# Cross-attention and MXFP8 FFN on one core: constants first, 8 warming matmuls, ScalarE's row statistics in halves, a later wait in the last down product, new orders

## The chip, the cores and the metric

One core of a Trainium2 chip runs the whole program. TensorE does the matmuls and reads instructions from its own queue, as do VectorE (DVE), ScalarE (ACT), GpSimd (POOL) and SyncE (SP), which issues most of the DMAs. The metric is the time of one execution on the device, in microseconds (us). The kernel before took 611.59 us (median of 3 runs, 611.04 to 611.65).

## The reference, cut to what matters

The input `x` is 4 x 512 x 512, the context 4 x 512 x 256, everything float32. A cross-attention without learned values is added to `x`, then a gated feed-forward network in which every matrix and every activation is rounded to float8 in blocks of 32 (quantised and dequantised):

```python
query = einsum('bnc,dc->bnd', ctx, Wq) + bq          # d = 128
key   = einsum('bnc,dc->bnd', ctx, Wk) + bk
attention = softmax(einsum('bnd,bmd->bnm', query, key), axis=-1)
x = x + einsum('bln,bmn->blm', layernorm(x), attention)

def mx_dequant(t):                                   # blocks of 32 along the last dimension
    scales = maximum(max_abs(blocks) / 448, 1e-30)
    return (blocks / scales).astype(float8_e4m3fn).astype(float32) * scales
def mx_linear(x2d, w): return mx_dequant(x2d) @ mx_dequant(w).T

gate, up = mx_linear(layernorm(x), gate_w), mx_linear(layernorm(x), up_w)   # 512 -> 2048
out = x + mx_linear(silu(gate) * up, down_w)                                # 2048 -> 512
```

## The kernel before, in words

**Stages.** The attention runs per batch entry b = 0..3 in 128-row tiles. `project(b, i)` makes queries (i = 0) or keys (i = 1) with 2 float32 matmuls; a float32 matmul stands in the profile as 2 records. `energies(b, nt)` makes one 128x512 tile of scores with 1 matmul. DVE's `row_max` and ACT's `exponential` turn it into unnormalised probabilities; `row_sum(b)` inverts the four sums; ACT's `weigh(b, nt)` scales an identity matrix by them. `turn_probs(b, nt)` multiplies the probabilities by that diagonal, which transposes and normalises them (4 matmuls, 128 columns each); `take_probs` copies the result to SBUF. `attend(b, lt)` multiplies by the rows of `x` (4 matmuls, 512 columns), and DVE's `add_attended` adds it to `x`, using the layernorm statistics that ACT makes in `row_means(b)` and `row_variances(b)`. The second layernorm is `attended_means` (DVE), `attended_variances` (ACT), a centring by DVE (`center`) or ACT (`center_by_scalar`), and `rows_scale`, `rows_round`, `rows_dequant` (DVE).

The weights come as 12 units of 1 MB: units 0 to 7 are gate and up for 4 column groups c, units 8 to 11 are the down matrix. Each is rounded by DVE (`unit_reduce`, `unit_scale`, `unit_round`, `unit_dequant`) with help of ACT (`unit_magnitude`, `unit_rescale`), and split into a high and a low float16 part: ACT writes the high part (`unit_hi`), GpSimd's accumulating DMA (`unit_rest`) forms the remainder, ACT writes the low part (`unit_lo`), and SP's transposing DMAs (`turn_unit_hi`, `turn_unit_lo`) put both in place. The normalised rows go the same way (`rows_hi`, `rows_rest`, `rows_lo`, `turn_rows_hi`, `turn_rows_lo`), and so do the hidden rows.

`product(r, c)` makes gate and up of row tile r (0..15) and column group c, in three float16 passes each (high x high, high x low, low x high): 24 matmuls. ACT's `silu_of` and DVE's `hidden_of` combine them. `down(r)` makes an output tile with 48 matmuls. `down_last()` makes tile 15 in two halves of 256 columns, so that the first half can be added and stored while the second is computed.

**What sets the order.** No planner runs with the kernel: each engine's instructions stand in an order written out by hand in the source, and an engine runs them strictly in this order. Semaphores hold an instruction back until its inputs are there; whatever stands behind it on that engine waits as well. The 8 PSUM banks are shared by a written list, `bank_uses`: a bank's next user waits until its last user has been read (`take_bank`, `bank_left`).

**Start.** DVE writes a block of zeros. TensorE runs `keep_zeros(18)` (L758): 18 float16 matmuls of those zeros into a spare bank. It then waits for both constant DMAs (L331 weights and biases, L332 identity) and for the context. SP issues in this order: the two halves of unit 0 (L325, L328), context 0 (L335), the two constant DMAs, context 1, unit 1, rows 0, context 2, unit 2, context 3, columns 0 and so on.

**End.** `down_last()` waits for both the high part (`hT_in[0]`) and the low part (`hT_in[1]`) of row 15 before its first matmul, then computes all of half 0 and all of half 1. DVE's `add_last` (L1612) and `store_last` (L364) follow each half.

Of the kernel before, what the change touches and what calls it, by code (L numbers as in the profile page):

```python
# [9 lines left out]
ALU = mybir.AluOpType  # L10
# [3 lines left out]
P = 128  # L14
# [18 lines left out]
def xattn_ffn(nc, xrows, xcols, ctxT, consts, units, out):  # L33
# [35 lines left out]
        ("p0.0 p2.0 t0.0 e2.1 a1.3 t3.3 a3.2 u3.1 g4.1 u6.2 u0.1 g1.1 g4.2 u7.1 d1 u13.0 g13.3 g8.3 g10.3 u15.0"  # L69
         " u15.3").split(),  # L70
        ("p0.1 e1.0 t0.2 e2.2 t2.0 e3.2 t3.1 g0.0 g2.1 u4.0 g3.2 g0.2 u0.3 u3.3 g7.2 g8.0 g9.1 u9.3 d3 u10.3 g15.1"
         " d10 d13").split(),
        ("p1.0 e1.1 a0.0 a0.2 t1.1 t1.3 a1.2 a2.2 u1.0 g6.0 u4.1 u3.2 g5.3 u1.1 g4.3 u7.2 g8.1 g9.2 u11.0 g12.0"
         " g14.0 g14.2 g12.2 u13.1 g12.3 g10.1 g11.3 d8 d11").split(),
        ("e0.0 e1.2 a0.1 a0.3 e3.1 t3.0 g1.0 a3.3 u2.1 g5.0 g5.1 u0.2 g1.2 u4.2 g7.3 u8.0 u9.1 g11.0 g11.2 g12.1"
         " u14.0 g14.3 g13.0 u13.2 u8.2 u10.2 d6 d9 d12").split(),
        ("e0.1 p2.1 t0.1 t0.3 e2.3 t2.1 e3.3 t3.2 a3.0 g2.0 g6.1 g2.2 u5.1 u5.3 u1.2 g7.0 g2.3 g9.0 g9.3 g11.1 d4"
         " u15.1 d14").split(),
        ("e0.2 e1.3 t1.0 t1.2 a1.1 t2.3 a2.1 u3.0 g3.1 u6.1 g6.2 g0.1 u6.3 g3.3 g7.1 u2.3 u9.0 g10.0 u11.1 u12.0"
         " g14.1 u14.2 u12.2 g13.2 u12.3 u10.1 u11.3 g15.2 d15").split(),  # L80
        ("e0.3 p3.0 e3.0 a2.3 a3.1 u2.0 g4.0 u2.2 u5.2 g0.3 u1.3 u7.0 d0 u10.0 u11.2 u12.1 u14.1 u14.3 g13.1 u13.3"
         " u8.3 d5 d7 g15.3").split(),
        ("p1.1 e2.0 p3.1 a1.0 t2.2 a2.0 g3.0 u0.0 u6.0 u5.0 g5.2 g6.3 g1.3 u4.3 u7.3 u8.1 u9.2 d2 g8.2 g10.2 g15.0"
         " u15.2").split(),
# [4 lines left out]
    logged = (0,)  # L89
    hidden_by_vector = (7, 8, 9, 10, 11, 12, 13, 14, 15)  # L90

    with ExitStack() as stack:
# [55 lines left out]
        idf = late[:, 1540:1540 + P]  # L148
        xsum, xnmean, xssq, xlog, xrstd, nmax, esum, rsum = [late[:, 1680 + RT * n:1680 + RT * (n + 1)] for n in range(8)]
        xTf = [h[:, 0:LT, 1536:2048], h[:, 0:LT, 1024:1536]]  # L150
# [22 lines left out]
        def hrow(r):  # L173
            return h[:, r % SLOTS, :]

# [34 lines left out]
        xmean_ready = sem("xmean_ready")  # L210
        ymean_ready = sem("ymean_ready")
# [106 lines left out]
        def _(sp):  # L318
# [121 lines left out]
            load_ctx(3)  # L440
            load_columns(0)
            load_rows(1)
            load_rows(2)
            load_columns(1)
# [3 lines left out]
            load_rows(3)  # L448
            load_unit(3)
            store_rows(0)  # L450
            load_columns(2)
# [20 lines left out]
            turn_rows_lo(1)  # L472
            turn_unit_hi(4)
            turn_unit_lo(4)
# [21 lines left out]
            turn_unit_hi(10)  # L496
            reload_rows(2)
            turn_unit_lo(10)
            turn_unit_hi(11)
            sp.wait_ge(*hidden_rest_in(0))  # L500
            turn_unit_lo(11)
            turn_hidden_hi(0)
# [9 lines left out]
            turn_hidden_hi(2)  # L512
            turn_hidden_hi(3)
            turn_hidden_lo(2)
            sp.wait_ge(*hidden_rest_in(4))
            turn_hidden_lo(3)
            sp.wait_ge(*rows_rest_in(3))
            turn_hidden_lo(4)
            turn_hidden_hi(4)
            sp.wait_ge(*hidden_rest_in(5))  # L520
            turn_rows_lo(3)
            turn_rows_hi(3)
            turn_hidden_hi(5)
            turn_hidden_lo(5)
            sp.wait_ge(*hidden_rest_in(6))
            turn_hidden_hi(6)
            turn_hidden_lo(6)
            turn_hidden_hi(7)
            turn_hidden_lo(7)
            load_last()  # L530
            turn_hidden_hi(8)
            turn_hidden_lo(8)
            turn_hidden_hi(9)
            turn_hidden_lo(9)
            turn_hidden_hi(10)
            turn_hidden_lo(10)
            turn_hidden_hi(11)
            turn_hidden_lo(11)
            turn_hidden_hi(12)
            turn_hidden_lo(12)  # L540
            turn_hidden_hi(13)
            turn_hidden_lo(13)
# [12 lines left out]
        def _(pool):  # L555
# [34 lines left out]
            unit_max(0)  # L590
            unit_max(1)
            unit_rest(0)
# [4 lines left out]
            unit_rest(2)  # L597
            unit_max(3)
            rows_rest(0)
            pool.wait_ge(wT_in[1], 48)  # L600
            unit_rest(3)
            unit_max(4)
            second_norm(1)
            pool.wait_ge(wT_in[1], 64)
            rows_rest(1)
            unit_rest(4)
            unit_max(5)
            pool.wait_ge(wT_in[1], 80)
            unit_rest(5)
            unit_max(6)  # L610
            pool.wait_ge(wT_in[1], 96)
            unit_rest(6)
            unit_max(7)
            unit_max(8)
            pool.wait_ge(wT_in[1], 112)
            unit_rest(7)
            unit_max(9)
            pool.wait_ge(wT_in[1], 128)
            unit_rest(8)
# [1285 lines left out]
```

## Time and profile before

| | us |
|---|---|
| median of 3 runs | 611.59 |
| the profiled execution itself | 611.49 |
| its span, first to last instruction | 609.7 |
| TensorE busy | 602.0 (99%) |
| DVE busy | 485.4 (80%) |
| ACT busy | 308.9 (51%) |
| GpSimd busy | 48.8 (8%) |

The span is 1.8 us shorter than the execution's time: that difference lies around the program's own instructions. Busy shares are means over stages with very different loads, so they are read by stretches of time. The granted TensorE clock is shown as full over the whole span.

### The profile page before, as it was taken

How to read it: one execution, taken by the hardware profiler on the slowest of the kernel's cores; microseconds unless marked ns; L12 is line 12 of the kernel's file. 1: busy time of each engine (PE TensorE's matmuls, PEld its weight loads, DVE VectorE, ACT ScalarE, POOL GpSimd, SP SyncE). 2: the span in 40 equal slices, each digit the busy share in tenths (PEclk: the TensorE clock that was granted, in tenths of full speed). 3: DMA queues.
4: the chain of work that ended last, by engine and by line, in shares of the span. 5: the costliest groups of instructions: out<-in, count | busy, mean ns of one | idle time of the engine just before them, and what ended most of it. 6: DMA issues, size and time to landing. Idle time of an engine off the chain costs nothing.

```text
span 609.7 us, 7213 instructions
## 1 busy us (share of the span) xinstructions
PE 602.0 (99%) x2690; PEld 282.8 (46%) x2690; DVE 485.4 (80%) x455; ACT 308.9 (51%) x463; POOL 48.8 (8%) x60
## 2 busy tenths in 40 slices
PE   8999999999999999999999999999999999999998
PEld 3455545444444444444444444444444444444446
DVE  5998998899999979899899997231148989799940
ACT  3989989553455545863572642421212512644521
POOL 0000100201100100102001100000000000110000
PEclk9999999999999999999999999999999999999999
DMA  8967989989888868775566668600110452856681
GB/s 326 384 144 263 293 229 213 258 216 250 207 206 207 209 135 176 172 158 130 130 118 140 162 140 147 137 4 15 18 19 0 90 86 51 137 90 102 119 141 34
DMA packets 148162, 92.28 MB, mean 151 GB/s; under 512 B 134304, under 2 KB 134688, under 8 KB 143264
## 3 DMA queue, kind: packets, MB, share of 16 engines
q1 hardware_dynamic: 142656, 63.78, 44.5%
q0 software_dynamic: 5472, 28.05, 19.8%
q8 instruction: 21, 0.34, 0.2%
q14 instruction: 13, 0.11, 0.1%
HBM read 25.76 MB, written 8.39 MB: 56 GB/s over the span
## 4 chain that ended last, share of the span: by engine, by line
PE 89%; ACT 7%; DMA 2%; issue 1%; SPq 0%; DVE 0%; DVEq 0%; ACTq 0%
PE bank L713 54%; PE bank L725 17%; PE bank L728 8%; PE bank L697 5%; PE bank L744 2%; ACT h L952 1%; DMA W<-hT 1%; PE bank L688 1%; ACT h L943 1%; PE bank L673 1%; DMA gu_lo<-in_consts 1%; PE bank L681 1%; ACT hT L932 1%; ACT mag L908 1%; ACT hT L994 0%
## 5 line engine op out<-in xcount | busy, mean ns | idle before, releaser
L713 PE MATMUL bank<-gu_hi,xT 128*128 128x512 f16 x1024 | 243.5, 379 | 1.0 <-DVE gu_hi L1440 1.0
L713 PEld LDWEIGHTS bank<-gu_hi,xT 128*128 128x128 f16 x1024 | 100.1, 98 | 122.2 <-issue 1.8
L713 PE MATMUL bank<-gu_lo,xT 128*128 128x512 f16 x512 | 131.4, 379 | 0.0
L725 PE MATMUL bank<-dn,hT 128*128 128x512 f16 x480 | 106.0, 379 | 0.0
L1569 DVE SCALAR_TENSOR_TENSOR h<-bank,unscale,silu 128x512 f32<-128x512 f32 x64 | 47.1, 747 | 58.8 <-PE bank L713 50.7
L1049 ACT ACTIVATE silu<-bank,unscale 128x512 f32<-128x512 f32 x64 | 42.9, 679 | 91.0 <-PE bank L713 38.3
L713 PEld LDWEIGHTS bank<-gu_lo,xT 128*128 128x128 f16 x512 | 50.1, 98 | 60.4
L725 PEld LDWEIGHTS bank<-dn,hT 128*128 128x128 f16 x480 | 47.0, 98 | 56.6
L1075 ACT ACTIVATE W<-h 128x2048 f16<-128x2048 f32 x16 | 30.6, 1911 | 65.7 <-issue 19.9
L697 PE MATMUL bank<-dn,h 128*128 128x512 f32 x128 | 56.0, 593 | 0.0
L728 PE MATMUL bank<-dn,hT 128*128 128x512 f16 x240 | 54.2, 379 | 0.0
L908 ACT ACTIVATE mag<-h 128x2048 bf16<-128x2048 f32 x18 | 34.3, 1907 | 33.5 <-DVE h L1583 18.9
L1404 DVE SCALAR_TENSOR_TENSOR h<-mag,h 128x2048 f32<-128x2048 bf16 x18 | 41.2, 2287 | 4.7 <-ACT mag L908 4.7
L1405 DVE SCALAR_TENSOR_TENSOR h<-mag,h 128x2048 f32<-128x2048 bf16 x18 | 41.3, 2292 | 0.6
L1595 DVE TENSOR_TENSOR h<-h,hscale 128x2048 f32<-128x2048 f32 x16 | 36.6, 2287 | 5.0 <-ACT hscale L1057 4.7
L697 PEld LDWEIGHTS bank<-dn,h 128*128 128x128 f32 x128 | 24.2, 190 | 30.0 <-issue 29.7
L1583 DVE TENSOR_TENSOR h<-h,rscale 128x2048 f32<-128x2048 f32 x16 | 36.7, 2292 | 0.5
L1578 DVE TENSOR_REDUCE hscale<-h 128x64 f32<-128x2048 f32 x16 | 36.5, 2280 | 0.4
L728 PEld LDWEIGHTS bank<-dn,hT 128*128 128x128 f16 x240 | 23.5, 98 | 28.3
L908 ACT ACTIVATE mag<-W 128x2048 bf16<-128x2048 f32 x14 | 26.7, 1904 | 15.9 <-DVE W L1526 12.8
L1404 DVE SCALAR_TENSOR_TENSOR W<-mag,W 128x2048 f32<-128x2048 bf16 x14 | 32.0, 2288 | 3.0 <-ACT mag L908 2.8
L1405 DVE SCALAR_TENSOR_TENSOR W<-mag,W 128x2048 f32<-128x2048 bf16 x14 | 32.1, 2292 | 0.5
(115 smaller groups left out, 552.8 us busy)
## 6 DMA issues: line engine op xcount, KB each, us to landing
W<-hT POOLq DMA_DIRECT2D x12, 1024.0 KB, 5.8
W<-in_units SPq DMA_DIRECT2D x11, 1024.0 KB, 6.0
h<-W POOLq DMA_DIRECT2D x7, 1024.0 KB, 5.8
h<-in_xcols SPq DMA_DIRECT2D x4, 1024.0 KB, 13.2
out_y<-y POOLq DMA_DIRECT2D x15, 256.0 KB, 4.9
h<-in_xrows SPq DMA_DIRECT2D x2, 1024.0 KB, 14.8
out_y<-h SPq DMA_DIRECT2D x2, 1024.0 KB, 7.7
h<-hT POOLq DMA_DIRECT2D x2, 1024.0 KB, 6.0
```

Source lines behind the costliest of these rows:

```text
L697: last = pe.matmul(bank[:, :], xTf[b % 2][:, j, lt * P:(lt + 1) * P], AT[:, j, :], start=(j == 0), stop=(j == HT - 1))
L713: last = pe.matmul(bank[:, :], xT[:, b % 2, part, k, :], w[:, c, g, j * 512:(j + 1) * 512], start=(j == 0 and not low), stop=(j == HT - 1 ...
L725: pe.matmul(bank[:, :], hT[:, r % 2, 0, k, :], dn[:, w, k, :], start=(k == 0 and w == 0), stop=False)
L728: last = pe.matmul(bank[:, :], hT[:, r % 2, 1, k, :], dn[:, 0, k, :], start=False, stop=(k == IT - 1))
L908: nc.scalar.activation(mag[:, :], v, ACT.Abs, scale=MAGIC).then_inc(mag_ready, 1)
L1049: nc.scalar.activation(silu[:, n % 2, :], bank_of(f"g{r}.{c}")[:, :], ACT.Silu, scale=unscale[:, 2 * c:2 * c + 1]).then_inc(silu_ready, 1)
L1404: then(dve.scalar_tensor_tensor(v, mag[:, :], floor, v, ALU.max, ALU.add))
L1405: dve.scalar_tensor_tensor(v, mag[:, :], floor, v, ALU.max, ALU.subtract).then_inc(mag_used, 1)
L1569: dve.scalar_tensor_tensor(hrow(r)[:, c * 512:(c + 1) * 512], bank_of(f"u{r}.{c}")[:, :], unscale[:, 2 * c + 1:2 * c + 2], silu[:, n % 2, ...
L1578: then(dve.tensor_reduce(s, blocks(row), AX.X, ALU.max, apply_absolute_value=True))
L1583: dve.tensor_tensor(blocks(row), blocks(row), each_block(rscale[:, :]), ALU.mult).then_inc(hv_ready, 1)
L1595: dve.tensor_tensor(blocks(row), blocks(row), each_block(hscale[:, r % 2, :]), ALU.mult).then_inc(hd_ready, 1)
```

## The change

The program computes the same thing. SP issues one DMA for all constants, then context 0, and the two halves of unit 0 after them. TensorE multiplies 8 blocks of zeros instead of 18. ACT's `row_means`, `row_variances`, `attended_variances` and `center_by_scalar` are called in halves of two row tiles, so that other work can stand between them. The centring of rows 1 moves from ACT to DVE. A DVE version of the statistics (`row_stats`) is added but called nowhere (`stats_by_vector = ()`). One `keep("t1.2", 6)` is added on TensorE: 6 float32 matmuls of the identity by itself, 128 columns each. `down_last()` waits for the low part after the high part's matmuls of both halves. The orders on all five engines and the bank list are rewritten; the core of the diff follows.

```diff
-        idf = late[:, 1540:1540 + P]
+        idf = late[:, 1538:1538 + P]
             def load_consts():
-                sp.dma_start(wts, consts[:, 0:514]).then_inc(consts_in, 16)
-                sp.dma_start(idf, consts[:, 514:514 + P]).then_inc(consts_in, 16)
+                sp.dma_start(late[:, 1024:1538 + P], consts).then_inc(consts_in, 16)
...
+            load_consts()
+            load_ctx(0)
             load_half(0)
             load_rest(0)
-            load_ctx(0)
-            load_consts()
             load_ctx(1)
             load_unit(1)
             load_rows(0)
+            load_ctx(3)
             load_ctx(2)
+            load_columns(0)
             load_unit(2)
...
             turn_unit_hi(3)
             turn_unit_lo(3)
+            turn_rows_hi(1)
             load_unit(6)
             store_rows(3)
             sp.wait_ge(*unit_rest_in(4))
-            turn_rows_hi(1)
             turn_rows_lo(1)
...
             def down_last():
                 r = RT - 1
-                bank = take_bank(f"d{r}")
+                halves = [take_bank(f"d{r}")]
                 pe.wait_ge(hT_in[0], 16 * (r + 1))
-                pe.wait_ge(hT_in[1], 16 * (r + 1))
                 for part in range(2):
                     cols = slice(part * H // 2, (part + 1) * H // 2)
                     if part == 1:
                         pe.wait_ge(down_taken, r)
-                        bank = bank_of(f"d{r - 1}")
+                        halves.append(bank_of(f"d{r - 1}"))
                     for k in range(IT):
-                        for a, w in ((0, 0), (0, 1), (1, 0)):
-                            last = pe.matmul(bank[:, cols], hT[:, r % 2, a, k, :], dn[:, w, k, cols],
-                                             start=(k == 0 and a + w == 0), stop=(k == IT - 1 and a == 1))
+                        for w in range(2):
+                            pe.matmul(halves[part][:, cols], hT[:, r % 2, 0, k, :], dn[:, w, k, cols],
+                                      start=(k == 0 and w == 0), stop=False)
+                pe.wait_ge(hT_in[1], 16 * (r + 1))
+                for part in range(2):
+                    cols = slice(part * H // 2, (part + 1) * H // 2)
+                    for k in range(IT):
+                        last = pe.matmul(halves[part][:, cols], hT[:, r % 2, 1, k, :], dn[:, 0, k, cols],
+                                         start=False, stop=(k == IT - 1))
                     last.then_inc((half_ready, down_ready)[part], 1)
...
-            keep_zeros(18)
-            pe.wait_ge(consts_in, 32)
+            keep_zeros(8)
+            pe.wait_ge(consts_in, 16)
```

The new order on TensorE from the start to the first products:

```text
p0.0 p0.1 p1.0 e0.0 e0.1 p1.1 e0.2 e0.3 e1.0 e1.1 e1.2 p2.0 t0.0-t0.3 e1.3 p2.1 p3.0
a0.0 a0.1 e2.0 e2.1 a0.2 a0.3 t1.0 p3.1 t1.1 keep(6) t1.2 e2.2 e2.3 t1.3
a1.0 e3.0 e3.1 e3.2 t2.0 a1.1 a1.2 a1.3 t2.1 t2.2 t2.3 e3.3
a2.0 a2.1 a2.2 t3.0 t3.1 a2.3 t3.2 t3.3 product(3,0) product(1,0)
a3.0 a3.1 a3.2 product(0,0) product(2,0) a3.3 product(3,1) product(2,1) product(6,0) ...
```

(p = project, e = energies, t = turn_probs, a = attend.) Before, product(0,0) stood ahead of a3.0, and product(2,0) behind a3.3. On ACT, new order around the same stretch:

```text
exp1.2 exp1.3 take_projection(3,0) row_means(1,0) row_means(1,1) unit_lo(0) weigh(1,0) weigh(1,1)
unit_rescale(1) row_variances(1,0) unit_magnitude(2) unit_hi(1) weigh(1,2) take_probs(1,0) (1,1) (1,2)
weigh(1,3) row_means(2,0) exp2.0 take_probs(1,3)
...
exp3.3 row_means(3,1) weigh(3,0) unit_magnitude(3) weigh(3,1) row_variances(3,0) weigh(3,2) weigh(3,3)
rows_lo(0) row_variances(3,1) unit_rescale(3) take_probs(3,0) (3,1) unit_lo(2) attended_variances(1,0)
take_probs(3,2) unit_hi(3) attended_variances(1,1) silu_of(3,0) take_probs(3,3) rows_magnitude(1)
```

On DVE, `add_attended(3,0)` moves ahead of `rows_dequant(1)`, `unit_reduce(5)`, `unit_round(4)` and `unit_dequant(4)`, behind which it stood, and `center(1)` is added behind `add_attended(2,1)`. Further on, `down` products shift by one to three products (down(4) behind product(12,1), down(8) and down(9) and product(15,3) earlier), with ACT, DVE and SP reordered to match.

## Rows read from the trace of the kernel before

**Rows 1.** TensorE's waits: who released it, us in total, times, longest.
```profile
PE bank L673 <- DMA gu_lo<-in_consts: 1.5, 1, 1.5
...
PE bank L713 <- DVE gu_hi L1440: 1.0, 1, 1.0
PE bank L688 <- ACT h L968: 0.8, 1, 0.8
```

**Rows 2.** Stretch: busy us of PE, PEld, DVE, ACT, POOL; clock, DMA, GB/s.
```profile
20.00:71.60 51.60, 50.61 (x164) 25.53 (x162) 48.79 (x55) 49.54 (x117) 2.40 (x3) 1.00 0.84 257
```

**Rows 3.** Timeline of TensorE, start to 109.8: start, us, instruction, count.
```profile
1.18 6.21 PE L758 MATMUL bank<-dn 128*128 128x512 f16 x18 [1.18 <-DVE dn L1616]
8.88 5.42 PE L673 MATMUL bank<-gu_hi,gu_lo 128*128 128x512 f32 x12 [1.49 <-DMA gu_lo<-in_consts]
...
76.94 13.90 PE L697 MATMUL bank<-dn,h 128*128 128x512 f32 x32
90.67 3.73 PE L688 MATMUL bank<-h,gu_lo 128*128 128x128 f32 x32
94.24 1.03 PE L713 MATMUL bank<-gu_hi,xT 128*128 128x512 f16 x4
...
109.78 13.90 PE L697 MATMUL bank<-dn,h 128*128 128x512 f32 x32
```

**Rows 4.** Timeline of the weight loads of the zeros, same columns.
```profile
5.00 0.15 PEld L758 LDWEIGHTS bank<-dn 128*128 128x128 f16 x1 [0.28 <-issue]
5.42 0.15 PEld L758 LDWEIGHTS bank<-dn 128*128 128x128 f16 x1 [0.28 <-issue]
5.72 1.18 PEld L758 LDWEIGHTS bank<-dn 128*128 128x128 f16 x6
```

**Rows 5.** Timeline of DVE at the start: reduces of unit 0's halves.
```profile
4.65 1.22 DVE L1505 TENSOR_REDUCE scale<-W 128x32 f32<-128x1024 f32 x1 [3.52 <-DMA W<-in_units]
6.28 1.22 DVE L1510 TENSOR_REDUCE scale<-W 128x32 f32<-128x1024 f32 x1 [0.41 <-DMA W<-in_units]
```

**Rows 6.** SP issues context 1, in its timeline; then issue to landing.
```profile
3.32 0.48 SPq L335 DMA_DIRECT2D gu_hi<-in_ctxT  x1
...
DMA to landing us min/median/max: 7.1/7.1/7.1
```

**Rows 7.** Timeline of ACT: one instruction of each kind in question.
```profile
52.14 1.06 ACT L975 ACTIVATE dn<-bank 128x512 f32<-128x512 f32 x2
...
61.69 0.68 ACT L962 ACTIVATE gu_lo<-bank,gu_lo 128x512 f32<-128x512 f32 x1
...
65.43 0.62 ACT L943 ACTIVATE h<-dn 128x512 f32<-128x512 f32 x1
...
71.04 0.97 ACT L968 ACTIVATE h<-gu_lo 128x128 f32<-128x128 f32 x3
```

**Rows 8.** Timeline of ACT: centring of rows 1, last copies of probabilities.
```profile
96.00 2.54 ACT L1021 ACTIVATE h<-h,nmean 128x512 f32<-128x512 f32 x4
...
105.78 1.07 ACT L975 ACTIVATE dn<-bank 128x512 f32<-128x512 f32 x2
```

**Rows 9.** SP turns the low part of rows 0; then issue to landing.
```profile
90.82 1.45 SPq L410 DMA_TRANSPOSE xT<-hT  x1
...
DMA to landing us min/median/max: 4.4/4.4/4.4
```

**Rows 10.** Timeline of DVE: the first sum of batch entry 3.
```profile
123.80 0.74 DVE L1440 SCALAR_TENSOR_TENSOR gu_hi<-bank,gu_lo,gu_hi 128x512 f32<-128x512 f32 x1
```

**Rows 11.** The end: TensorE, ACT, SP in their timelines; last row's landing time.
```profile
596.08 10.64 PE L744 MATMUL bank<-dn,hT 128*128 128x256 f16 x96
...
596.28 1.50 ACT L1092 ACTIVATE y<-bank,xnmr,odown 128x128 f32<-128x128 f32 x4 [8.85 <-PE bank L728]
...
587.80 2.26 SPq L429 DMA_TRANSPOSE hT<-W  x1
...
DMA to landing us min/median/max: 6.9/6.9/6.9
```

More of the change, by code:

```diff
@@ L174, in hrow, with means_made @@
             return h[:, r % SLOTS, :]
+        def means_made(b):
+            return 1 + sum(n not in stats_by_vector for n in range(b))
         def of(b):
@@ L998, in attended_variances @@
                                                     accum_out=ysum[:, row])
-                act.wait_ge(act_step, own.done(last))
+                own.done(last)
+                if half == 0:
+                    return
+                act.wait_ge(act_step, own.n)
                 if b in logged:
@@ L1112, in _ @@
             exponential(0, 3)
-            take_projection(1, 1)
-            row_means(0)
-            row_variances(0)
-            take_projection(2, 0)
+            row_means(0, 0)
             weigh(0, 0)
-            take_projection(2, 1)
-            exponential(1, 0)
             weigh(0, 1)
             weigh(0, 2)
+            unit_rescale(0)
+            take_probs(0, 0)
+            weigh(0, 3)
+            row_means(0, 1)
+            take_probs(0, 1)
+            take_probs(0, 2)
@@ L1122, in _ @@
+            take_probs(0, 3)
+            take_projection(2, 0)
+            exponential(1, 0)
+            row_variances(0, 0)
+            unit_magnitude(1)
             unit_hi(0)
-            take_probs(0, 0)
-            take_probs(0, 1)
-            weigh(0, 3)
-            take_probs(0, 2)
             exponential(1, 1)
-            take_probs(0, 3)
-            unit_magnitude(1)
+            take_projection(2, 1)
+            row_variances(0, 1)
             exponential(1, 2)
             exponential(1, 3)
-            unit_rescale(1)
+            take_projection(3, 0)
@@ L1133, in _ @@
+            row_means(1, 0)
+            row_means(1, 1)
             unit_lo(0)
             weigh(1, 0)
-            row_means(1)
-            row_variances(1)
             weigh(1, 1)
+            unit_rescale(1)
+            row_variances(1, 0)
             unit_magnitude(2)
-            exponential(2, 0)
+            unit_hi(1)
             weigh(1, 2)
-            unit_hi(1)
             take_probs(1, 0)
             take_probs(1, 1)
-            unit_rescale(2)
-            weigh(1, 3)
-            take_projection(3, 0)
@@ L1147, in _ @@
-            take_projection(3, 1)
-            take_probs(1, 2)
-            take_probs(1, 3)
-            attended_variances(0)
-            exponential(2, 1)
-            unit_lo(1)
+            take_probs(1, 2)
+            weigh(1, 3)
+            row_means(2, 0)
+            exponential(2, 0)
+            take_probs(1, 3)
+            exponential(2, 1)
+            unit_rescale(2)
             exponential(2, 2)
             exponential(2, 3)
+            take_projection(3, 1)
+            weigh(2, 0)
@@ L1155, in _ @@
+            unit_lo(1)
+            row_means(2, 1)
+            attended_variances(0, 0)
+            weigh(2, 1)
             rows_magnitude(0)
-            row_means(2)
-            row_variances(2)
-            weigh(2, 0)
-            weigh(2, 1)
+            attended_variances(0, 1)
+            row_variances(1, 1)
+            unit_hi(2)
+            exponential(3, 0)
             weigh(2, 2)
-            unit_hi(2)
             weigh(2, 3)
@@ L1164, in _ @@
             take_probs(2, 1)
+            exponential(3, 1)
             take_probs(2, 2)
@@ L1167, in _ @@
             rows_hi(0)
-            exponential(3, 0)
-            exponential(3, 1)
+            row_variances(2, 0)
+            row_variances(2, 1)
             exponential(3, 2)
+            row_means(3, 0)
             exponential(3, 3)
-            unit_lo(2)
+            row_means(3, 1)
             weigh(3, 0)
@@ L1175, in _ @@
             weigh(3, 1)
+            row_variances(3, 0)
             weigh(3, 2)
@@ L1178, in _ @@
             rows_lo(0)
-            row_means(3)
-            row_variances(3)
+            row_variances(3, 1)
             unit_rescale(3)
             take_probs(3, 0)
-            center_by_scalar(1)
             take_probs(3, 1)
+            unit_lo(2)
+            attended_variances(1, 0)
+            take_probs(3, 2)
+            unit_hi(3)
+            attended_variances(1, 1)
             silu_of(3, 0)
-            unit_hi(3)
-            attended_variances(1)
-            take_probs(3, 2)
             take_probs(3, 3)
@@ L1667, in _ @@
             row_max(3, 2)
+            rows_dequant(0)
+            add_attended(1, 0)
+            add_attended(1, 1)
+            unit_reduce(3)
+            add_attended(1, 2)
             row_max(3, 3)
+            unit_largest(3)
+            add_attended(1, 3)
             unit_scale(3)
+            attended_means(1)
             row_sum(3)
-            add_attended(1, 3)
+            add_attended(2, 0)
             unit_reduce(4)
-            attended_means(1)
+            unit_power(3)
```

595 lines of the change are left out of this document (308 added, 287 removed).

## The prediction

> **What bounds the kernel now.** I read the table of busy times first: TensorE is busy for 602.0 of 609.7 us. The matmuls that must be done hardly change, so only three things can move the time: when TensorE's real work starts, the idle time inside it, and what follows its last matmul. The list of its waits [rows 1] puts a size on the second: 1.5 us for the constants ahead of the first projection, then 0.8 us for a diagonal (L968), 1.0 us for the sum of x and attention (L1440), and nothing over 0.2 us else. From 125 us to the end TensorE never waits. So the gain can come only from before 125 us, and the reordering behind that can only cost.
>
> The timeline of TensorE [rows 3] then gives the places: zeros from 1.18, first projection at 8.88, first product at 94.24. Real work takes, per record, 13.73 / 32 = 0.429 us for 512 float32 columns (76.94 to 90.67) and 3.57 / 32 = 0.112 us for 128 columns (90.67 to 94.24). Between 8.88 and 94.24 stand 160 records of the first kind (32 of projections, 32 of energies, 96 of attend) and 128 of the second: 68.7 + 14.3 = 83.0 us in 85.4. So 2.4 us were idle there, of which the list names about 1; the rest is gaps too short to be shown. The stretch view shows why idle time can return: from 20 to 71.6 us ACT is busy 49.5 of 51.6 us and DVE 48.8 [rows 2]. Three engines are full at once.
>
> **The start.** DVE's two reduces begin as the halves of unit 0 land, at 4.65 and 6.28 [rows 5]: 512 KB take 1.63 us, so the first one began to move at about 3.0. In the new order 321 KB of constants (1.0 us) and 512 KB of context 0 come first and land near 5.65. The first projection moves from 8.88 to 5.65: 3.2 us. That isn't the gain, though. TensorE's third projection needs context 1, which landed at 3.32 + 7.1 = 10.4 [rows 6] and has exactly the same bytes ahead of it in both orders. I take 10.3 (10.0 to 10.5; one merged constants DMA in place of two may save a little). Before, this projection began at 8.88 + 8 x 0.438 = 12.4 (x12 records in 5.26 us [rows 3]). So the front is worth at most 12.4 - 10.3 = 2.1 us, and TensorE idles about 1.2 us ahead of it.
>
> Fewer zeros cost clock. The zeros' weight loads are 0.42 us apart up to 5.42, and the last six take 1.18 us together, 0.2 each [rows 4]; 512 columns in 0.427 us is the 1.2 GHz level, in 0.213 the 2.4 GHz level (the granted clock is recorded as full for both). The rise came at 5.72, after 4.5 us of multiplying. The 8 zeros end at 1.18 + 8 x 0.427 = 4.6, and 1.05 us of idle follow. Lower bound of the cost: the clock rises by the time context 0 is there, or rises late inside the idle time ahead of context 1: 0. Upper bound: the count starts anew at 5.65 and the slow level holds for 4.5 us, to 10.2: 5.3 of the 8 records of two projections at 0.857 us, 2.7 at 0.43, end 11.35 in place of 10.3: 1.05 us. The new kernel has 3.4 us of zeros behind it, so I take the middle, 0.5. The third projection begins at 10.8; the front is worth 1.6 us (1.05 to 2.1).
>
> The Trainium skill (TensorE: Matmul & The Clock Gate, Part 1: The HAM clock gate) says that the array starts at the slow level and that how many matmuls run slowly differs between runs of one kernel, since the monitor does not start with the kernel; by that rule the cost lies anywhere between my two ends from run to run. Its quick reference advises a longer warm-up than 8 zeros give, which speaks against this edit and would make the start 10.3 to 11.35, as above. Whether a break resets the clock no row here shows.
>
> **From context 1 to the first product.** Before, 12.4 to 94.24 is 81.8 us; the work in it is 83.0 - 3.4 = 79.6, idle 2.2. New terms:
> - `keep("t1.2", 6)`: 12 records of 128 columns at 0.112: +1.3 us. If TensorE would have waited there for ACT it is free; following the queues I find that weigh(1,2) is done about as TensorE comes to it, so I count it in full.
> - attend(1,0) waits for take_probs(1,3). Behind turn_probs(1,2), ACT has take_probs(1,2) 0.5, weigh(1,3) 0.3, half of row_means(2) 1.25, an exponential 0.67, take_probs(1,3) 0.5, 3.2 us, and about 0.4 for two handovers [rows 7]. TensorE has energies(2,2), (2,3) and turn_probs(1,3): 4 x 0.43 + 0.9 = 2.6. Wait: 1.0 (0 to 2).
> - turn_probs(3,1) needs weigh(3,1), which stands behind a magnitude (1.8 us) behind weigh(3,0): about 0.5 (0 to 1.5).
> - Other short gaps: 0.4; before, they were over 1.
> The 0.8 us wait for L968 goes: row_variances(2) now stands behind the weighing it used to hold up. Sum: 79.6 + 1.3 + 1.0 + 0.5 + 0.4 = 82.8; first product at 93.6, 0.6 us ahead of 94.24.
> Cutting the statistics into halves costs ACT nothing: the same instructions run. What it gives is that no weighing or copy stands behind 5.5 us of statistics.
>
> A floor lies under this. The low part of rows 0 landed at 90.82 + 4.4 = 95.2 [rows 9]; the first product's third pass needs it 1.73 us (8 matmuls) after its start, at 95.97 before. ACT's `rows_lo(0)` comes at about the same time in the new queue (behind four weighings that wait for row_sum(3)). So TensorE can gain at most 0.7 us up to here, whatever the front gives; with 93.6 + 1.7 = 95.3 the two meet.
>
> **The products.** Before, product(2,0) waited 1.0 us for add_attended(3,0) at 123.80 [rows 10], which stood behind a whole round and dequant of unit 4 on DVE. It now stands three such blocks earlier, and two products lie between attend(3,0) and its user: -1.0 us. In return attend(3,0) comes one product (5.2 us) earlier: 94.24 + 3 x 5.18 = 109.8 [rows 3] becomes about 104, and needs take_probs(3,3), which ended at 105.78 + 1.07 = 106.85 [rows 8]. ACT no longer centres rows 1 (2.45 us [rows 8]) and does row_means(3) earlier, so take_probs(3,3) should end near 103.7. Cost taken: 0; bounds 0 to 2.8. center(1) costs DVE 1.6 us, hidden behind TensorE's products, and rows_dequant(1) still ends some 2 us earlier than before. Turning rows 1 high before store_rows(3) only helps: product(6,0) had about 1 us of slack. The later moves of down products lengthen the distance between a hidden row's turn and its use: 0, covered by products of 5.18 us each.
>
> **The end.** The low part of row 15 landed at 587.80 + 6.9 = 594.7, before down_last began at 596.1 [rows 11]: the later wait removes nothing (0), it only adds 7 us of cover. Half 0 is complete 1.7 us before the end in place of 5.2; its two adds and its store still go out ahead of half 1's. Half 1's matmuls need take_down(14) 3.5 us after down_last starts (5.2 before); it took 0.2 + 1.5 [rows 11]. Cost 0, at most 0.2 if the two stores meet.
>
> **Sum.** -0.6 (start to first product) -1.0 (product(2,0)) = -1.6, against the profiled execution of 611.49 (span 609.7 and 1.8 around it): 609.9. The median of runs is 0.1 above it, and so I say 610.0.
>
> **The rivals.**
> - *ScalarE gives it back* (36%). ACT has 2 us free in 51.6 [rows 2], and half a dozen handovers at which I allow only 0.2 us. If weighings and copies come 1 us later than I think, or the clock costs its full 1.05, the first product starts at 94.24 as before. For it: three engines are full, and keep(6) is pure addition. Against: the 0.8 us wait was just such a block and is gone. Only the 1.0 remains at best: 610.5 to 611.6, about 611.0.
> - *attend(3,0) too early for ACT* (12%, slower). take_probs(3,3) still stands behind attended_variances(1), unit_hi(3) and the first silu. If ACT is no earlier than before, TensorE waits 106.85 - 104 = 2.8 us there; with the 1.6 gained, 611.49 - 1.6 + 2.8 = 612.7. It costs from the point where take_probs(3,3) ends after 104, and turns the sign from 105.6. Against: 2.45 us of centring left ACT.
> - *All of the front arrives* (inside the forecast): clock cost 0, no wait at attend(1,0), rows_lo(0) 1 us earlier: 608.8.
> - That the late wait or the zeros don't do what they say changes nothing beyond the above.
>
> **How the numbers follow.** A measurement of this kernel can tell 0.2%, 1.2 us. My forecast, 52%, spans 608.8 to 610.3. The ScalarE rival is within 0.2% (36%), the third case slower (12%). Range 608.7 to 612.3: it leaves out the worst of the slower case and little below.
>
> **What would show it.** First projection near 5.7, third near 10.3 to 11.4; zeros all 0.43 apart; a first product at 93.3 to 94; no wait for L1440 at product(2,0); attend(3,0) without a wait over 0.3; no wait of TensorE behind 130 us; 3.0 us from the last matmul to the end, unchanged. Wrong if the list of waits names ACT with more than 3 us in total, or any hidden or unit transfer behind 130 us.

## The result, and the profile after

The changed kernel takes 614.65 us (median of 4 runs, 614.52 to 615.5), the kernel before 611.62 us (4 runs, 611.04 to 612.67). The ratio is 1.0049, 95% interval 1.0037 to 1.0062: it is slower, by 3.0 us, where 610.0 was forecast. The profiled execution took 614.74 us, with a span of 612.8 us (before: 611.49 and 609.7) and a granted clock of 1.0. Beside each run the profiler lists the clock that TensorE was granted, as a mean over the run: three of the four runs have 1.0 (614.52 to 614.74 us), the one of 615.5 has 0.997.

First TensorE's waits (releaser, us in total, times, longest), to be laid beside [rows 1]:

```profile
PE bank L700 <- ACT dn L1001: 2.6, 2, 1.7
PE bank L676 <- DMA gu_hi<-in_ctxT: 1.7, 2, 0.9
PE bank L746 <- ACT y L1122: 1.6, 1, 1.6
PE bank L766 <- DVE dn L1669: 1.2, 1, 1.2
PE bank L691 <- ACT h L994: 0.2, 1, 0.2
```

The wait for L1440 is gone, as forecast, and of the one for L968 0.2 us are left (L994 in the new kernel). New are two for contexts at the projections (L676), two at `attend` (L700) for copies of probabilities (0.9 us in attend(1,0), 1.7 in attend(3,0)), and one at the second half of `down_last` (L746) for an output row. The timeline of TensorE (start, us, instruction, count, idle before) puts them in place. It answers to [rows 3] and to the first row of [rows 11]:

```profile
1.18 3.60 PE L766 MATMUL bank<-dn 128*128 128x512 f16 x8 [1.18 <-DVE dn L1669]
5.66 5.30 PE L676 MATMUL bank<-gu_hi,gu_lo 128*128 128x512 f32 x8 [0.89 <-DMA gu_hi<-in_ctxT]
11.77 1.99 PE L676 MATMUL bank<-gu_hi,gu_lo 128*128 128x512 f32 x4 [0.80 <-DMA gu_hi<-in_ctxT]
...
49.85 1.50 PE L760 MATMUL bank<-gu_lo 128*128 128x128 f32 x12
...
55.75 2.81 PE L700 MATMUL bank<-dn,h 128*128 128x512 f32 x6 [0.90 <-ACT dn L1001]
...
88.41 1.13 PE L691 MATMUL bank<-h,gu_lo 128*128 128x128 f32 x8 [0.15 <-ACT h L994]
...
94.60 1.03 PE L716 MATMUL bank<-gu_hi,xT 128*128 128x512 f16 x4
...
107.02 10.54 PE L700 MATMUL bank<-dn,h 128*128 128x512 f32 x24 [1.74 <-ACT dn L1001]
...
131.19 1.03 PE L716 MATMUL bank<-gu_hi,xT 128*128 128x512 f16 x4
...
597.39 3.66 PE L746 MATMUL bank<-dn,hT 128*128 128x256 f16 x32
602.67 3.67 PE L746 MATMUL bank<-dn,hT 128*128 128x256 f16 x32 [1.63 <-ACT y L1122]
606.18 3.66 PE L752 MATMUL bank<-dn,hT 128*128 128x256 f16 x32
```

Against before, the first product starts 0.4 us later (94.60 for 94.24). The product at 131.19 stood at 129.88 in the kernel before (the second four of a group of eight records that starts at 129.01), with the same work ahead of it apart from `keep`: 1.3 us later. From there to `down_last` both kernels take 466.2 us (597.39 - 131.19, and 596.08 - 129.88). `down_last` ends at 609.84 in place of 606.72: 3.1 us later. So the 3.1 us of the span are 0.4 up to the first product, 0.95 from there to 131 us, and 1.8 in `down_last`; against the forecast they are 1.0, 1.9 and 1.8.

**attend(3,0).** ACT's timeline, to be laid beside [rows 8]:

```profile
98.45 0.58 ACT L1001 ACTIVATE dn<-bank 128x512 f32<-128x512 f32 x1
100.83 1.91 ACT L935 ACTIVATE hT<-W 128x2048 f16<-128x2048 f32 x1 [1.81 <-issue]
102.65 0.70 ACT L1020 ACTIVATE hT<-h,nmean 128x512 f32<-128x512 f32 x1
...
104.41 1.28 ACT L1079 ACT_TABLE_LOAD   x1
105.70 0.69 ACT L1079 ACTIVATE silu<-bank,unscale 128x512 f32<-128x512 f32 x1
106.29 0.59 ACT L1001 ACTIVATE dn<-bank 128x512 f32<-128x512 f32 x1
```

The copy at 98.45 is take_probs(3,2). The next one, take_probs(3,3), is done at 106.88. Before, it was done at 106.85 [rows 8]. Between the two copies stand `unit_hi(3)` (L935), ahead of which ACT idles 1.81 us, a half of the statistics (L1020), the load of silu's table, and a silu. The profile names no releaser for the idle time before L935 ("issue"), but the code does: `unit_hi(3)` writes over the part of hT that SP's transpose of unit 2's high part reads, and waits for its end (`wT_in[0]`). That transpose is issued here and lands 6.9 us later, at 100.7, 0.1 us before L935 starts:

```profile
93.83 2.82 SPq L391 DMA_TRANSPOSE gu_hi<-hT  x1
...
DMA to landing us min/median/max: 6.9/6.9/6.9
```

In the kernel before it was issued at 92.32, 1.5 us earlier, and ACT came to `unit_hi(3)` only at 100.92 and did not wait. So the new orders bring ACT to it earlier and the transfer to it later.

**down_last.** ACT's timeline in the last 25 us, beside the second line of [rows 11], and GpSimd's issues of the stores of finished rows:

```profile
588.78 1.91 ACT L1105 ACTIVATE W<-h 128x2048 f16<-128x2048 f32 x1 [7.09 <-DVE h L1648]
590.60 1.49 ACT L1122 ACTIVATE y<-bank,xnmr,odown 128x128 f32<-128x128 f32 x4
...
592.45 1.51 ACT L1122 ACTIVATE y<-bank,xnmr,odown 128x128 f32<-128x128 f32 x4 [0.17 <-ACT odown L1095]
...
597.48 1.51 ACT L1122 ACTIVATE y<-bank,xnmr,odown 128x128 f32<-128x128 f32 x4 [3.35 <-DMA out_y<-y]
...
601.11 1.51 ACT L1122 ACTIVATE y<-bank,xnmr,odown 128x128 f32<-128x128 f32 x4 [1.75 <-DMA out_y<-y]
```

```profile
592.40 0.87 POOL L589 DMA_DIRECT2D out_y<-y  x1 [11.12 <-ACT y L1122]
594.32 0.86 POOL L589 DMA_DIRECT2D out_y<-y  x1 [1.05 <-ACT y L1122]
599.28 0.86 POOL L589 DMA_DIRECT2D out_y<-y  x1 [4.10 <-ACT y L1122]
602.99 0.89 POOL L589 DMA_DIRECT2D out_y<-y  x1 [2.85 <-ACT y L1122]
```

The four L1122 groups are take_down(11) to take_down(14). TensorE had finished the first two at about 566 and 577 us, but in ACT's new order they are behind `hidden_hi(15)`, which waits 7.09 us for DVE. `y`, from which the finished rows are stored, has two buffers. So take_down(13) must wait for the store issued at 592.40 (landed 5.0 us later, 597.4), and take_down(14) for the one issued at 594.32 (6.7 us, 601.0). TensorE needs the bank that take_down(14) frees at 601.0 and gets it at 602.6. In the kernel before, take_down(14) ran at 596.28, without any store in its way.

The low part of row 15 is also later: its transpose (L434) is issued at 593.60 and lands 7.6 us later, at 601.2, against 594.7 before [rows 11]. DVE's timeline shows where that begins: in the new order row 14 is itself later. Its low part (first line) starts at 578.53 after a wait of 1.98 us for ACT, where it started at 574.00 before, and row 15's steps stand behind it:

```profile
578.53 2.29 DVE L1654 SCALAR_TENSOR_TENSOR W<-h,W 128x2048 f16<-128x2048 f32 x1 [1.98 <-ACT W L1105]
581.80 2.29 DVE L1447 SCALAR_TENSOR_TENSOR h<-mag,h 128x2048 f32<-128x2048 bf16 x1 [0.98 <-ACT mag L917]
584.13 2.29 DVE L1448 SCALAR_TENSOR_TENSOR h<-mag,h 128x2048 f32<-128x2048 bf16 x1
586.46 2.29 DVE L1648 TENSOR_TENSOR h<-h,hscale 128x2048 f32<-128x2048 f32 x1
```

### The profile page after: what moved, and what is told of

It is laid out like the page before. It is cut to its first block, busy times and chain, and to the rows that moved or that the text cites. A ratio compares the mean times of both kernels' runs of the same rounds, so it can differ in the third digit from the quotient of the medians.

```text
span 612.8 us, 7235 instructions
## 1 busy us (share of the span) xinstructions
PE 602.5 (98%) x2692; PEld 283.7 (46%) x2692; DVE 485.4 (79%) x459; ACT 306.7 (50%) x459; POOL 47.9 (8%) x60
## 4 chain that ended last, share of the span: by engine, by line
PE 43%; issue 38%; ACT 6%; DMA 6%; DVE 3%; POOL 2%; SPq 1%; ACTq 0%; DVEq 0%; POOLq 0%
PE bank L716 26%; PE bank L700 7%; PE bank L728 2%; PE bank L684 2%; PE bank L676 2%; PE bank L691 2%; DMA gu_hi<-in_ctxT 1%; POOL out_y L589 1%; DMA hT<-W 1%; DMA W<-W 1%; PE bank L731 1%; DMA out_y<-y 1%; DVE h L1636 1%; DVE hscale L1631 1%; DVE h L1447 1%
## 5 line engine op out<-in xcount | busy, mean ns | idle before, releaser
L700 PE MATMUL bank<-dn,h 128*128 128x512 f32 x128 | 56.5, 594 | 2.6 <-ACT dn L1001 2.6
L1654 DVE SCALAR_TENSOR_TENSOR W<-h,W 128x2048 f16<-128x2048 f32 x9 | 20.6, 2290 | 26.3 <-DMA hT<-W 22.3
L700 PEld LDWEIGHTS bank<-dn,h 128*128 128x128 f32 x128 | 24.0, 190 | 31.9 <-issue 29.9
L1447 DVE SCALAR_TENSOR_TENSOR W<-mag,W 128x2048 f32<-128x2048 bf16 x14 | 32.0, 2288 | 2.7 <-ACT mag L917 2.7
```

The costliest lines, as they stand in the source:

```text
L700: last = pe.matmul(bank[:, :], xTf[b % 2][:, j, lt * P:(lt + 1) * P], AT[:, j, :], start=(j == 0), stop=(j == HT - 1))
L1447: then(dve.scalar_tensor_tensor(v, mag[:, :], floor, v, ALU.max, ALU.add))
```

## The experiments

Twelve kernels ran, each timed beside the kernel before, whose median in the groups was 611.62 to 611.69. The mean granted clock of each run is on record, and it matters: in the kernels that begin with 8 zeros it was 0.997 or less in 37 of 80 runs, in those with 18 zeros in none of 39 and in none of the runs of the kernel before. In each of those kernels the runs at the lower clock took longer, by 0.7 to 2.8 us between the two groups' medians. So a median depends on how often that happened, and the runs at 0.999 to 1.0 are compared where it changes a reading. Those named a_ and c_ are built on the changed kernel, those named b_ on the kernel before.

**a_take_early.** The copies of rows 11 and 12 ahead of `hidden_hi(15)` in ACT's order:

```diff
             hidden_magnitude(15)
-            hidden_hi(15)
             take_down(11)
             hidden_unscale(12)
             take_down(12)
+            hidden_hi(15)
```

> The changed kernel with take_down(11), hidden_unscale(12) and take_down(12) ahead of hidden_hi(15) on ScalarE. Theory: TensorE's 1.6 us wait inside the last down product is a chain through the two output buffers y: take_down(11) stands behind hidden_hi(15), so its store goes out at 592, take_down(13) waits for that store's landing and take_down(14) for the next one (601.0), past the time at which TensorE needs it. With the takes moved the wait vanishes: 614.65 - 1.6 = 613.0. Rival: the low part of row 15, which landed at 601.2, or another transfer takes its place: 614.0 to 614.7.

612.34 us (12 runs, 611.43 to 614.46), 1.0018 (1.0007 to 1.003). The wait is gone from `down_last`; its timeline:

```profile
596.29 7.15 PE L746 MATMUL bank<-dn,hT 128*128 128x256 f16 x64
603.27 3.66 PE L752 MATMUL bank<-dn,hT 128*128 128x256 f16 x32
```

The gain is 2.3 us, of which this wait is 1.6 to 1.8. The rest is the start: in the profile context 1 landed at 10.65 in place of 11.73, which this edit doesn't touch (below). The wait in `down_last` and its cause in ACT's order are shown.

**a_probs_early.** take_probs(3,3) directly behind take_probs(3,2):

```diff
             take_probs(3, 2)
+            take_probs(3, 3)
             unit_hi(3)
             attended_variances(1, 1)
             silu_of(3, 0)
-            take_probs(3, 3)
```

> The changed kernel with take_probs(3,3) directly behind take_probs(3,2) on ScalarE, ahead of unit_hi(3), the second half of attended_variances(1) and the first silu with its table load. Theory: TensorE's 1.7 us wait at attend(3,0) is that queue's doing: the copy would end near 99.5 in place of 106.8, and the wait vanishes: 614.65 - 1.7 = 612.9. Rival: what stood behind the wait (rows 1, units 4 and 5) is late as well and TensorE waits there instead: 613.8 to 614.7, with new waits behind 107 us.

613.04 us (6 runs, 612.06 to 614.7), 1.0028 (1.0016 to 1.0041): 1.6 us less than the changed kernel. attend(3,0) starts without a wait, at the very end of the product ahead of it, and the one in `down_last` stays at 1.4 us:

```profile
104.56 1.03 PE L716 MATMUL bank<-gu_hi,xT 128*128 128x512 f16 x4
105.43 2.74 PE L700 MATMUL bank<-dn,h 128*128 128x512 f32 x6
```

**a_both.** Both edits.

> Both moves together. Theory: the two waits are independent and add: 614.65 - 3.3 = 611.3, level with the kernel before. Rival: one of them hides the other, since a TensorE that is 1.7 us ahead needs the hidden rows at the end earlier: 612.5 to 613.5.

610.51 us (12 runs, 609.83 to 612.87), 0.999 (0.9979 to 1.0002): 4.1 us less than the changed kernel, where the two edits alone gave 2.3 and 1.6. The two add up. But 0.8 us of the 4.1 belong to neither by the profile: context 1 landed 0.8 us earlier, and the first product starts at 93.83 in place of 94.60. The edits' own share, some 3.3 us, is the whole loss of 3.0 and little more. attend(3,0) starts at 104.36, without a wait.

**a_old_last.** The changed kernel with `down_last` as before, one wait for both parts of row 15:

```diff
-                halves = [take_bank(f"d{r}")]
+                bank = take_bank(f"d{r}")
                 pe.wait_ge(hT_in[0], 16 * (r + 1))
+                pe.wait_ge(hT_in[1], 16 * (r + 1))
...
-                            pe.matmul(halves[part][:, cols], hT[:, r % 2, 0, k, :], dn[:, w, k, cols],
+                        for a, w in ((0, 0), (0, 1), (1, 0)):
+                            last = pe.matmul(bank[:, cols], hT[:, r % 2, a, k, :], dn[:, w, k, cols],
```

> The changed kernel with the last down product as before: it waits for the high and the low part at its start and computes half 0 completely, then half 1. Theory: the new form of this product needs take_down(14) 1.7 us earlier than the old, but in the new order the low part of row 15 lands at 601.2, 3.6 us after the product's start, so the old form waits 3.6 us at its start and nothing inside: 614.65 - 1.6 + 3.6 = 616.6. Rival: the landing at 601.2 was a chance of transfers meeting and is normally near 595: then the old form has neither wait, 613.0.

617.63 us (6 runs, 615.31 to 619.78), 1.0096 (1.0075 to 1.0117): 3.0 us more than the changed kernel, where 2.0 more had been expected. `down_last` begins when the low part of row 15 is there, and then runs slowly at first. Its line in the timeline, and the stretch behind its start, with TensorE's granted clock in the third column from the right:

```profile
601.16 12.31 PE L747 MATMUL bank<-dn,hT 128*128 128x256 f16 x96 [3.61 <-DMA hT<-W]
```

```profile
601.00:605.00 4.00, 3.83 (x24) 2.95 (x25) 0.00 (x0) 1.48 (x4) 0.89 (x1) 0.69 0.60 86
```

The 96 records take 12.3 us, and 10.6 in the kernel before [rows 11]: behind the idle 3.6 us the granted clock was 0.69, which is 1.7 of the 3.6 us that this profile is longer. The wait for the low part is 3.6 more and the one that goes is 1.6 less. Two of the six runs had a mean clock of 1.0: 615.31 and 615.6, 0.9 us above the changed kernel's runs at 1.0 (614.57). The four others took 617.14 to 619.78. So the new form is worth 0.9 us where the clock held, and 2.6 to 5.2 where it did not. Why the first figure is 0.9 and not 2.0 is not shown.

**b_new_last.** The opposite: the kernel before, with the new `down_last` alone.

> The kernel before with the new last down product alone. Theory: there the low part of row 15 had landed at 594.7, before the product began, and take_down(14) took 2.0 us of the 3.5 that the new form allows: no change, 611.6. Rival: the two stores of the last row, now 1.7 us apart, meet: 611.9 to 612.2.

611.62 us (11 runs, 610.69 to 612.41), 0.9997 (0.9989 to 1.0006). The late wait is worth nothing where the row lands at 594.7, and 0.9 us or more where the new orders of ACT and DVE make it land at 601. It repairs part of what another part of the same change breaks.

**b_front.** The kernel before, with the new start alone: constants in one DMA, context 0 behind them, then the halves of unit 0; 8 zeros.

```diff
+            load_consts()
+            load_ctx(0)
             load_half(0)
             load_rest(0)
-            load_ctx(0)
-            load_consts()
             load_ctx(1)
...
-            keep_zeros(18)
+            keep_zeros(8)
...
```

> The kernel before with the new start alone: one constants DMA and context 0 ahead of the halves of unit 0, and 8 zeros. Theory: there DVE's first row_max stands behind unit_reduce(1), and unit_scale(0) ends 2.6 to 4 us later with the new loads; the first exponential moves from 15.9 to about 18, and ScalarE is the full engine from 20 to 72 us, so this start alone makes the kernel before slower, by 1 to 2 us: 613.2. Rival: TensorE's earlier start is what counts, 611.0 or below.

612.42 us (11 runs, 611.56 to 613.81), 1.0017 (1.0008 to 1.0025): slower by 0.75 us. Nine of its runs had a mean clock of 0.997 or less; the two others took 612.08 (the profiled one) and 612.26, 0.5 more than the kernel before. TensorE's waits:

```profile
PE bank L680 <- ACT xT L937: 1.7, 2, 1.2
PE bank L757 <- DVE dn L1615: 1.2, 1, 1.2
PE bank L712 <- DVE gu_hi L1439: 1.0, 1, 1.0
PE bank L687 <- ACT h L967: 0.8, 1, 0.8
PE bank L672 <- DMA gu_hi<-in_ctxT: 0.7, 1, 0.7
```

TensorE now waits 1.7 us at its energies (L680) for projections that ACT has yet to copy (`xT`), and the first product starts at 94.87, 0.6 later than before. In the old orders ScalarE gives the earlier start back, and more; the 1 to 2 us that I had expected were too many.

**c_old_front.** a_both with the start of the kernel before (halves first, two DMAs of constants, 18 zeros).

> The kernel with both moves, with the start of the kernel before: halves of unit 0 first, then context 0, two constants DMAs, context 1; 18 zeros. It tells what the new start is worth in its own orders. Theory: the third projection starts at 12.4 in place of 11.0 to 12.0, and with it all of TensorE's queue: 610.5 + 0.9 = 611.4. Rival: DVE has unit 0 scaled 2.5 to 4 us earlier, the first row_max is not held up, and the old start is as good or better: 610.0 to 610.5.

612.8 us (11 runs, 612.49 to 613.24), 1.0017 (1.0008 to 1.0025): 2.3 us more than a_both, where 0.9 had been expected. By the profiles 1.3 of it is the first product, at 95.15 in place of 93.83, and 1.3 a wait for the low part of rows 0 (see c_18zeros). With the new orders the new start pays.

**c_18zeros.** a_both with 18 zeros.

```diff
-            keep_zeros(8)
+            keep_zeros(18)
```

> The kernel with both moves, with 18 zero matmuls in place of 8. Theory: context 1 landed at 11.7 and the two projections ahead of it ended at 10.9 even at the slow clock, so warming more saves nothing, and 18 zeros end near 7.4, in time: 610.5. Rival: the clock matters behind the wait for context 1, and warm matmuls give 0.5 to 1 us: 609.5 to 610.0. Other rival: the later first projection costs, 611.0 or more.

611.68 us (11 runs, 610.85 to 612.4), 1.0000 (0.9992 to 1.0009): 1.2 us more than a_both, against what I expected. The rival that allowed for 611.0 or more had the later first projection as its reason, and that isn't it: the extra zeros end at 7.8, and the first product starts at 93.76, as in a_both (93.83). The profile's loss is elsewhere, in one wait for the low part of rows 0, whose transfer took 5.6 us here and 4.35 in a_both:

```profile
PE bank L716 <- DMA xT<-hT: 1.3, 1, 1.3
```

c_old_front has the same wait (1.3 us). Between these two, with 18 zeros in both, the load order and the single DMA of constants are worth 1.1 us.

**c_no_keep.** a_both without the six idle multiplications (12 records) ahead of turn_probs(1,2).

```diff
             turn_probs(1, 1)
-            keep("t1.2", 6)
             turn_probs(1, 2)
```

> The kernel with both moves on ScalarE (610.5), without keep("t1.2", 6). Theory: in the changed kernel turn_probs(1,2) started at 51.19 behind the 1.34 us of these matmuls, while its diagonal was ready at 50.3, so 0.8 us of them are pure addition: 609.8. Rival: the first product is bound by the low part of rows 0 (landed 96.43 where it was wanted at 96.33), which ScalarE's queue sets, not TensorE's: 610.5, no change.

609.35 us (6 runs, 608.9 to 611.46), 0.9966 (0.9954 to 0.9979). The best of all kernels here: 1.2 us less than a_both and 2.3 less than the kernel before, and, with c_no_keep_18, one of only two that are faster than it by over 0.2%. Most of the 1.34 us of `keep` was on the path: 1.05 us by the runs at a clock of 0.999 to 1.0 (609.19 and 610.24), and little of it lay in a wait that TensorE would have had anyway. The profiled execution, at 611.46 the longest of its runs and the only one at 0.997, shows why they spread:

```profile
5.13 3.67 PE L676 MATMUL bank<-gu_hi,gu_lo 128*128 128x512 f32 x8 [0.35 <-DMA gu_hi<-in_ctxT]
11.54 3.43 PE L676 MATMUL bank<-gu_hi,gu_lo 128*128 128x512 f32 x4 [2.74 <-DMA gu_hi<-in_ctxT]
```

The first two projections ran at the upper clock level (0.46 us per record), so TensorE was done early and idled 2.74 us until context 1 was there; then four records took 3.43 us in place of 1.98: the lower level.

**c_no_keep_18.** c_no_keep with 18 zeros.

> Both moves on ScalarE, no keep(6), and 18 zero matmuls. With 18 zeros the kernel with both moves took 1.2 us more (611.7 against 610.5), and its profile shows a wait of 1.3 us for the low part of rows 0, whose transfer took 5.6 us where it took 4.4 in the profiles with 8 zeros. Theory: that is how this one program's transfers happened to meet, and the zeros themselves cost nothing: 609.4 and, as the clock stays up, fewer runs near 612. Rival: 18 zeros cost in the long run: 610.5 to 611.

609.76 us (6 runs, 609.32 to 610.53), 0.9969 (0.9957 to 0.998): the same as c_no_keep within 0.4 us, with less spread: all six runs had a clock of 1.0. The zeros end later, TensorE idles 0.2 us ahead of context 1, and the third projection is fast:

```profile
7.73 3.60 PE L676 MATMUL bank<-gu_hi,gu_lo 128*128 128x512 f32 x8
11.51 1.98 PE L676 MATMUL bank<-gu_hi,gu_lo 128*128 128x512 f32 x4 [0.18 <-DMA gu_hi<-in_ctxT]
```

The low part of rows 0 landed here in 4.35 us, without a wait. So c_18zeros lost by a transfer, not by its zeros. Against c_no_keep's five runs at 0.999 to 1.0 (609.19) 18 zeros cost 0.6 us, and they save the 2 us of the others.

**c_ctx1_first.** c_no_keep with context 1 ahead of unit 0's halves, and unit 0's steps on DVE and ACT behind the first row maxima and exponentials.

```diff
             load_ctx(0)
+            load_ctx(1)
             load_half(0)
             load_rest(0)
-            load_ctx(1)
...
```

> Both moves, no keep(6), 8 zeros; context 1 ahead of the halves of unit 0; on DVE row_max(0,0) and (0,1) ahead of unit_scale(0); on ScalarE unit_magnitude(0) behind the first two exponentials. Theory: the third projection no longer waits (11.0 to 12.0 becomes about 9), the attention starts 2 us earlier and half of it survives: 608.5. Rival: DVE, which gets unit 0 1.6 us later, is full from 20 us on and sets the rest, or the low part of rows 0 stays where it is: 609.4 to 611.

611.2 us (11 runs, 610.01 to 612.48), 0.9989 (0.998 to 0.9998): 1.9 us more than c_no_keep (1.2 by the runs at 0.999 to 1.0: 610.35 and 609.19). My hope failed. The rival had put the loss on DVE, which gets unit 0 later, or on rows 0, at 609.4 to 611. Context 1 landed at 8.44 and the energies began early, but TensorE then waits 2.1 us for ACT's diagonals, and ACT, in the second timeline, had waited for a row maximum of DVE:

```profile
23.83 5.44 PE L691 MATMUL bank<-h,dn 128*128 128x128 f32 x32 [2.11 <-ACT h L993]
```

```profile
20.73 0.69 ACT L987 ACTIVATE dn<-bank,gu_lo 128x512 f32<-128x512 f32 x1 [1.14 <-DVE gu_lo L1475]
```

That is the DVE rival in part. Besides, the 32 records behind the wait took 5.44 us in place of 3.73: the granted clock from 25 to 28 us was 0.56. The first product started at 96.10.

**c_copy_first.** c_no_keep with take_probs(1,3) ahead of exponential(2,0) on ACT, to remove the wait at attend(1,0).

```diff
+            take_probs(1, 3)
             exponential(2, 0)
-            take_probs(1, 3)
```

> Both moves, no keep(6), 8 zeros, and on ScalarE take_probs(1,3) ahead of exponential(2,0). In every kernel of the new order TensorE waits 0.9 us at attend(1,0) for that copy. Theory: the exponential takes 0.67 us of it, the wait shrinks to 0.2 and most of the gain lasts: 609.35 - 0.6 = 608.8. Rival: the low part of rows 0 is the floor ahead of the first products, as the prediction had it, and takes the gain back: 609.3 to 609.5, with a wait of TensorE for this transfer.

611.56 us (12 runs, 609.63 to 613.81), 0.9998 (0.9985 to 1.0011). The wait stayed, 0.84 us:

```profile
53.87 1.05 PE L691 MATMUL bank<-h,dn 128*128 128x128 f32 x8
55.76 0.67 PE L700 MATMUL bank<-dn,h 128*128 128x512 f32 x1 [0.84 <-ACT dn L1000]
```

Between turn_probs(1,3) and attend(1,0) TensorE has no other work. The copy can't begin before the turning ends (54.9) and takes 0.6 us; the handovers there and back are the rest. By these rows no order on ACT removes that: in the changed kernel too the copy began at 55.02, less than 0.2 us behind the end of the turning. Most of the 2.2 us that this kernel takes above c_no_keep is the clock. In its profile the third projection ran at the lower level (3.66 us for four records, after 2.14 us of idle), which is worth 1.7 us, and nine of its twelve runs have a mean clock of 0.997 or less, against one of six in c_no_keep. The three others took 609.63, 609.65 and 610.26, 0.5 us above c_no_keep's 609.19. Why the lower level came so much oftener here is open: the edit acts behind the start, and the two ran in different groups.

## Why the prediction was wrong

- **Start: sizes off by 1.0 us.** The first projection came at 5.66 (5.65 forecast). Context 1, taken to land at 10.3 since its bytes were the same, landed at 11.7, and in the other profiles of kernels with this start and load order at 10.65 to 12.03. "It has exactly the same bytes ahead of it in both orders" holds of the bytes and not of their rate: from 5 to 7 us the DMA engines moved 168 and 242 GB/s in the changed kernel, 240 and 387 in the kernel before. The clock's cost of 0.5 was 0 in this profile: the slow projections ended at 10.96, before the context landed. The third projection began at 11.77, not 10.8. Another cost of 8 zeros stood neither in the sum nor among the rivals: where the first two projections ran fast, TensorE idled longer ahead of context 1, and the clock could fall there (c_no_keep). The Trainium skill's advice to warm up longer, which the prediction names, stands in TensorE: Matmul & The Clock Gate, Why this matters for your kernels. The runs fit it: none of those with 18 zeros had a mean clock under 0.999.
- **To the first product: the sum right, its parts by luck.** The sum was 82.8 us from the third projection on; it took 94.60 - 11.77 = 82.8. `keep` took 1.34 us and c_no_keep gives 1.1 to 1.2 of them back, and of the wait for L968 0.2 was left. At turn_probs(3,1) TensorE waited 0.15 (0.5 forecast), so about 0.8 are short gaps (0.4 forecast). The wait at attend(1,0) was 0.9 (1.0 forecast), but not for the queue of ACT that the sum counted: with the exponential out of the way it was still 0.84 (c_copy_first). The floor lay where it was put: the low part of rows 0 landed at 92.09 + 4.35 = 96.4, 1.8 us after the first product's start, just as the third pass wanted it.
- **product(2,0): right.** Its wait of 1.0 us went.
- **attend(3,0): the first step that failed.** "take_probs(3,3) should end near 103.7" was a count of ACT's work alone. It ended at 106.9, since `unit_hi(3)` ahead of it waits for a transfer, and that transfer was issued 1.5 us later than before. This was the rival with 12%: 1.7 us in place of its 2.8. a_probs_early shows it.
- **The end: the second.** "Cost 0, at most 0.2 if the two stores meet" took take_down(14) to run as before, 0.2 + 1.5 us. I looked at that one copy and not at the queue ahead of it. Two earlier copies behind `hidden_hi(15)`, and stores of 5.0 and 6.7 us on two buffers, put it at 601.11. a_take_early shows it: 1.6 us of wait, 1.8 in all. No rival of mine had it.
- **The late wait.** "Removes nothing" is right for the kernel before (b_new_last) and wrong for the orders it came with: in a_old_last it is worth 0.9 us where the clock held, and more where the longer idle time brought it down.
- **Behind 130 us nothing waits** was right up to `down_last`, 466.2 us long in both.

Sum: 1.0 + 1.7 + 1.8 is 4.5 of the 4.65 us between forecast and result. With the two orders mended, a_both takes 610.5, and the forecast was 610.0. That is close in part because context 1 landed at 11.0 in its profile and not at 11.7. The gains that were counted were there, and two queues were not walked to their end.

## What to carry to other kernels

When an engine's order is rewritten, walk each later instruction on which TensorE waits back through its own queue until nothing ahead of it waits for someone else; the durations of the work in between are the lesser part. A copy that frees a bank or a buffer belongs ahead of an instruction that waits for another engine, never behind it. An edit at the start can also change how often the clock falls there, so compare the clock of every run and not only the medians. And a part of a change that measures as nothing in one order can be what holds another up: test each part in both.

## What the runs showed of the hardware

- Same queue order, different landing: context 1 landed between 10.65 and 12.03 us in the profiles of kernels with the new load order (10.4 in the kernel before, by [rows 6]). Between 5 and 6 us DMA moved 168 (changed kernel), 188 (c_no_keep) or 221 GB/s (a_both).
- The rise of the clock at the start fell differently in like kernels: after 8 zeros, eight records of the first projections took 5.30 and 5.52 us (changed kernel, a_probs_early) or 3.67 (a_take_early, a_both, c_no_keep, c_copy_first). The Trainium skill (TensorE: Matmul & The Clock Gate, Part 1: The HAM clock gate) says that the number of slow matmuls differs between runs of one kernel; these rows, of kernels alike up to there, fit it.
- After 2.74 and 2.14 us of idle the next four records took 3.43 and 3.66 us and the granted clock of the stretch from 10 to 20 us was 0.83; after 1.85 us (a_both) they took 1.98 us, at 1.00. So projections that ran fast could buy an idle stretch that was paid back in the next one. It also fell behind 2.11 us of idle at 24 us (c_ctx1_first, 0.56 from 25 to 28 us) and 3.61 us at 601 us (a_old_last, 0.69 from 601 to 605 us).
- The mean granted clock of a run was 0.997 or less in 37 of 80 runs that began with 8 zeros (four of them of a_old_last, whose profile shows the fall at its end) and in none of 39 that began with 18, where TensorE had 0.2 us or nothing to wait ahead of context 1 (c_no_keep_18, c_18zeros).
- The same transpose by DMA (low part of rows 0) took 4.35 us in most programs, and 5.6 to 5.7 in c_18zeros and c_old_front, in which TensorE then waited for it.
